# The first expert layer of a two-layer attention and mixture-of-experts kernel: another order of chunks, a selection in two parts, one more wait on GpSimd, and two one-hot matrices written by ScalarE

## The chip, the cores and the metric

The kernel runs on one core of a Trainium2 chip. The metric is the device time of one execution in microseconds (us). The engines are TensorE (PE; PEld is its loading of weights), VectorE (DVE), ScalarE (ACT), GpSimd (POOL) and SyncE (SP), which here only issues DMAs.

## What is computed

There are 2048 tokens (8 x 256) of width 256, and four layers, each added to its input after a layer norm: attention over sets, a mixture of 16 experts with a shared one, an attention over context, and a mixture of 8 experts. The second layer is the one that most of the change touches:

```python
scores = jax.nn.sigmoid(x @ router_w.T)                       # 2048 x 16
_, topk_idx = jax.lax.top_k(scores + e_bias[None, :], 4)
topk_w = jnp.take_along_axis(scores, topk_idx, axis=1)
topk_w = topk_w / (topk_w.sum(axis=-1, keepdims=True) + 1e-20)
combine = jnp.zeros((T, 16)).at[jnp.arange(T)[:, None], topk_idx].add(topk_w)
for each expert e:  g, u = split(x @ gu_w[e].T);  routed += combine[:, e] * (silu(g) * u @ d_w[e].T)
shared = silu(x @ shared_gate_w.T) * (x @ shared_up_w.T) @ shared_down_w.T
```

In the fourth layer each token goes to two of eight experts. The kernel computes for each choice a slot in a table of 39 blocks of 128 rows, and from that the list of the rows that each block gathers.

## The kernel before

**The first experts.** The 16 experts of width 96 are laid side by side, 1536 columns, and cut into 12 chunks of 128; the shared expert is a 13th chunk of 96 (`C0` = 13). Tokens go in four groups of 512 (`NG`). In `ffn0_group(g, k)` TensorE does for each chunk `c`: a small matmul that spreads the weights of the chosen experts over the chunk's 128 hidden rows (`spread`, into bank 4, L1108), then `up0` of the next chunk (12 matmuls of 512 columns, since each product is made of three, high x high, high x low and low x high: L1065 to L1067), then `down0` of this chunk (12 matmuls of 256 columns). Between `up0` and `down0` of a chunk stand ScalarE's silu (L806), VectorE's product with the up part (L1589), its product with the spread weights (L1594; not for the shared chunk, which comes last), the rounding to the high part (L1599) and the two halves of the low part (L1603).

**The weights of the choice.** Before the first group's loop VectorE chooses, in one row of 15 dependent steps, four of sixteen experts for all 16 tiles of 128 tokens (`dve.max`, `dve.match_replace`, normalising, and a split of each weight in three bf16 parts, `c3`; L1545 to L1574). TensorE, having done `up0(0, 0, 0)`, waits for that (`b_c3`), turns `c3` (16 transposes, L1121), ScalarE copies the four results (`cT`, L796), and only then does the loop start.

**Low parts of the weights and inputs.** GpSimd makes them (`gate_low`, `down_low0`, `low_rows`): L535, L548, L542. `GU_PART` and `DN_PART` say which columns go in which piece, in the order in which chunks need them.

**Weights of the last layer.** Beside the first experts the weights of the last layer are split in 68 parts of 512 columns: SyncE loads a part, ScalarE rounds it (`high_part`, L817), GpSimd subtracts (`low_part`, L577), SyncE stores both. ScalarE's order is fixed: in the first group parts 0 and 1 come behind the silu of chunk 0, part 2 behind that of chunk 1, part 3 behind that of chunk 2, parts 4 and 5 behind that of chunk 3. `high_part(n)` waits until the low part `n - 2` is made (`p_lo`) and the high part `n - 2` is stored (`hi_out`). GpSimd makes its first low part only behind all of the work of the paragraph above.

**Slots in the last layer.** For eight batches of four columns VectorE writes small matrices `placed` (L1777) and, in one instruction of 512 columns, four one-hot matrices (L1780); TensorE multiplies them (L1303). What it sums is the list by which GpSimd fetches rows (L667).

What sets the order is the program of each engine, written by hand; semaphores tie them.

## Time and profile before

| | us |
|---|---|
| median of 3 runs | 760.92 |
| lowest, highest | 759.76, 761.35 |
| the profiled execution | 759.37 |
| its span, first to last instruction | 757.6 |
| TensorE busy in it | 697.8 (92%) |
| VectorE, ScalarE, GpSimd busy | 480.2, 253.1, 332.3 |

The profiled execution is 1.8 us longer than its span, and 1.55 us shorter than the median. The first experts run from about 83 to 347 us of the span, the choice of slots from about 456 to 474 us, the last experts from 480 us to the end.

### The profile page before, as it was taken

The numbers are of one execution on the slowest core, as the hardware profiler recorded it, in microseconds if no ns is written. First come the engines' busy times: TensorE is split into PE (matmuls) and PEld (weight loads), VectorE is DVE, ScalarE is ACT, GpSimd is POOL, SyncE is SP. The second block draws the span as 40 slices with busy tenths as digits, with TensorE's granted clock in tenths as the row PEclk, the third lists the DMA queues.
The fourth block names the chain that finished last, engine by engine and source line by source line (L and its number), as shares of the span: only waits on it lengthen the run. The fifth ranks groups of instructions, "written<-read, shape, count | busy, mean of one in ns | idle before, by whom it ended". The sixth has DMA issues, their size and how long they took to land.

```text
span 757.6 us, 14725 instructions
## 1 busy us (share of the span) xinstructions
PE 697.8 (92%) x4707; PEld 622.5 (82%) x4707; DVE 480.2 (63%) x1322; ACT 253.1 (33%) x474; POOL 332.3 (44%) x324
## 2 busy tenths in 40 slices
PE   4999679999999999998899995699999999999996
PEld 3868558878888888887677784599999999999995
DVE  5969956667667677766699958344444444454443
ACT  1367233222322232335556640132323323233231
POOL 6236943434344334335512115345554655455553
PEclk9997569999999999999999995699999999999998
DMA  8901036766667766747950028522445355434221
GB/s 219 332 2 32 25 119 214 241 219 222 206 221 237 232 202 207 256 158 300 430 153 30 29 66 308 159 36 44 107 90 154 50 155 161 148 58 146 44 37 21
DMA packets 60265, 114.95 MB, mean 152 GB/s; under 512 B 15185, under 2 KB 29394, under 8 KB 57778
## 3 DMA queue, kind: packets, MB, share of 16 engines
q1 hardware_dynamic: 50514, 103.48, 40.1%
q0 software_dynamic: 8736, 10.39, 8.4%
q8 instruction: 37, 0.61, 0.3%
q10 hardware_dynamic: 960, 0.33, 0.2%
q14 instruction: 18, 0.15, 0.1%
HBM read 68.89 MB, written 45.29 MB: 151 GB/s over the span
## 4 chain that ended last, share of the span: by engine, by line
PE 78%; DVE 14%; issue 4%; ACT 2%; DMA 1%; POOLq 0%; POOL 0%; DVEq 0%
PE ps L1065 19%; PE ps L1066 18%; PE ps L1067 18%; PE ps L1335 3%; PE ps L1192 2%; PE ps L1183 2%; PE ps L1229 2%; PE ps L1108 1%; PE ps L937 1%; PE ps L1314 1%; PE ps L1205 1%; DVE h_high L1599 1%; DVE h_low L1603 1%; PE ps L1140 1%; PE ps L1221 1%
## 5 line engine op out<-in xcount | busy, mean ns | idle before, releaser
L577 POOL TENSOR_TENSOR part_lo<-wexp,part_hi 128x512 fp32r<-128x512 f32 x68 | 89.3, 1323 | 133.6 <-ACT part_hi L817 131.3
L684 POOL DMA_INDIRECT out_rows<-vbd,slot_row x39 | 63.3, 1623 | 107.4 <-DVE vbd L1819 75.7
L1065 PE MATMUL ps<-w_hi,x_high 128*128 x312 | 105.1, 337 | 1.1 <-DVE x_low L1824 1.1
L1066 PE MATMUL ps<-up_low,x_high 128*128 x312 | 101.6, 326 | 0.0
L1067 PE MATMUL ps<-w_hi,x_low 128*128 x312 | 101.6, 326 | 0.0
L1840 DVE TENSOR_TENSOR arena<-arena,ps 128x704 f32<-128x704 f32 x39 | 34.6, 888 | 103.1 <-ACT arena L905 86.9
L1065 PE MATMUL ps<-xn_high,gu_high 128*128 (+3 forms) x208 | 93.0, 447 | 0.1
L806 ACT ACTIVATE wexp<-ps 128x512 f32<-128x512 f32 (+1 forms) x52 | 31.1, 597 | 160.4 <-PE ps L1067 160.3
L1066 PE MATMUL ps<-xn_low,gu_high 128*128 (+3 forms) x208 | 82.9, 399 | 0.0
L1067 PE MATMUL ps<-xn_high,gu_low 128*128 (+3 forms) x208 | 82.7, 397 | 0.0
L517 POOL TENSOR_TENSOR rstd<-ve,mhalf 128x2 f32<-128x2 f32 (+1 forms) x31 | 22.3, 719 | 110.3 <-DVE ve L1397 110.3
L905 ACT ACTIVATE arena<-ps 128x704 f32<-128x704 f32 x39 | 29.6, 759 | 119.6 <-PE ps L1067 72.2
L1065 PE MATMUL ps<-dn_high,h_high 128*128 128x256 f32 (+1 forms) x208 | 61.3, 295 | 4.5 <-DVE h_low L1603 4.5
L1065 PEld LDWEIGHTS ps<-w_hi,x_high 128*128 128x128 f32 x312 | 59.8, 192 | 1.5 <-issue 1.5
L1065 PE MATMUL ps<-w_hi,hT_high 128*128 x195 | 58.7, 301 | 2.0 <-DVE hT_high L1833 2.0
L1589 DVE TENSOR_TENSOR wexp<-wexp,ps 128x512 f32<-128x512 f32 (+1 forms) x52 | 35.7, 686 | 39.0 <-ACT wexp L806 38.8
L1066 PEld LDWEIGHTS ps<-up_low,x_high 128*128 128x128 f32 x312 | 59.8, 192 | 0.0
L1067 PEld LDWEIGHTS ps<-w_hi,x_low 128*128 128x128 f32 x312 | 59.6, 191 | 0.0
L1066 PE MATMUL ps<-dn_low,h_high 128*128 128x256 f32 (+1 forms) x208 | 58.8, 283 | 0.0
L1067 PE MATMUL ps<-dn_high,h_low 128*128 128x256 f32 (+1 forms) x208 | 58.6, 282 | 0.0
L1603 DVE TENSOR_TENSOR h_low<-wexp,h_high 128x256 fp32r<-128x256 f32 (+1 forms) x104 | 55.4, 574 | 1.8
L1067 PE MATMUL ps<-w_hi,hT_low 128*128 x195 | 55.6, 285 | 0.0
(287 smaller groups left out, 1693.2 us busy)
## 6 DMA issues: line engine op xcount, KB each, us to landing
wexp<-in_wexp SPq DMA_DIRECT2D x68, 256.0 KB, 3.2
w_hi_rows<-part_hi SPq DMA_DIRECT2D x68, 256.0 KB, 2.6
w_lo_rows<-part_lo SPq DMA_DIRECT2D x68, 256.0 KB, 2.1
w_hi<-w_hi_rows SPq DMA_DIRECT2D x8, 2048.0 KB, 19.0
up_low<-w_lo_rows SPq DMA_DIRECT2D x8, 1408.0 KB, 6.0
down_low<-w_lo_rows SPq DMA_DIRECT2D x8, 768.0 KB, 8.3
wexp<-in_gu SPq DMA_DIRECT2D x2, 1632.0 KB, 10.8
xn_rows<-arena SPq DMA_DIRECT2D x8, 256.0 KB, 2.1
```

Source lines behind the costliest of these rows:

```text
L517: pool.tensor_tensor(rstd[:, bass.ds(b * TB, TB)], ve[:, bass.ds(b * TB, TB)], mhalf[:, 0:1].broadcast_to([P, TB]), ALU.pow).then_inc(ln_r ...
L577: pool.tensor_tensor(part_lo[:, n % 2, :], part_w[:, n % 4, :], part_hi[:, n % 2, :].bitcast(F32), ALU.subtract).then_inc(p_lo, 1)
L684: pool.indirect_dma_start(out=out_rows, out_offset=bass.IndirectOffsetOnAxis(ap=slot_row[:, i:i + 1], axis=0), in_=yb[:, i % 2, :], in_off ...
L806: act.activation(sg0[0:rows, c % 2, :], bank(c % 2)[0:rows, :], ACT.Silu).then_inc(b_silu, 1)
L905: act.activation(sg1.rearrange("p (a n) -> p a n", a=2), bank(0, 2).rearrange("p (a n) -> p a n", a=2)[:, :, 0:HALF1], ACT.Silu).then_inc( ...
L1065: pe.matmul(out, high, rows_high, start=start, stop=False, skip_group_check=True)
L1066: pe.matmul(out, high, rows_low, start=False, stop=False, skip_group_check=True)
L1067: return pe.matmul(out, low, rows_high, start=False, stop=stop, skip_group_check=True)
L1335: mm = pe.transpose(bank(4, 2)[:, c * P:(c + 1) * P], h1[:, c * P:(c + 1) * P], ident[:, :])
L1589: dve.tensor_tensor(hm0[0:rows_, c % 2, :], sg0[0:rows_, c % 2, :], bank(2 + c % 2)[0:rows_, :], ALU.mult).then_inc(b_prod, 1)
L1603: dve.tensor_tensor(h_low[0:rows_, c % 2, cols], hm0[0:rows_, c % 2, cols], h_high[0:rows_, c % 2, cols].bitcast(F32), ALU.subtract).then_ ...
L1840: dve.tensor_tensor(h1[:, 0:I1].rearrange("p (a n) -> p a n", a=2), sg1.rearrange("p (a n) -> p a n", a=2), bank(2, 2).rearrange("p (a n) ...
```

## The change

1. **Order of chunks.** In every group the shared chunk (96 rows, no weights) comes first, then experts' chunks 9, 10, 11, then 6 to 8, 3 to 5, 0 to 2 (`chunk_of`). `GU_PART`, `DN_PART` and `down_high0` follow that order: the first piece of the gate and up weights has 960 columns where it had 768, the last 768 where it had 960.
2. **Choice in two parts.** VectorE chooses for tiles 0 to 3 (group 0) ahead of the chunks; for the other twelve tiles the steps are put behind chunks 0 to 7 of group 0 (`select_rest`). TensorE turns the weights of group 0 behind `up0(0, 1)`, those of groups 1 and 2 behind chunk 8, those of group 3 behind chunk 10; ScalarE's copies are set in its row of silus.
3. **GpSimd** waits for the first part of the choice (`b_c3`) before it goes on with low parts.
4. **One-hots.** Those of batches 2 and 5 are made by ScalarE: four `Abs(inblock - iota)` of 128 columns and one `Relu(1 - .)` of 512.

**GpSimd between the norm and the first parts of the last layer's weights.** `xn_low`, `gu_low` and `dn_low` are the low parts; `part_lo` is the last layer's. Before:

```order
L542 TENSOR_TENSOR xn_low<-wexp,xn_high 128x2x256 [waits b_routed] x2
L535 TENSOR_TENSOR gu_low<-wexp,gu_high 128x960 [waits w_high]
L548 TENSOR_TENSOR dn_low<-wexp,dn_high 128x768 [waits w_high]
L535 TENSOR_TENSOR gu_low<-wexp,gu_high 128x960 [waits w_high]
L548 TENSOR_TENSOR dn_low<-wexp,dn_high 128x768 [waits w_high]
L542 TENSOR_TENSOR xn_low<-wexp,xn_high 128x2x256 [waits b_routed] x3
L577 TENSOR_TENSOR part_lo<-wexp,part_hi 128x512 [waits p_hi] x2
```

and now:

```order
L554 TENSOR_TENSOR xn_low<-wexp,xn_high 128x2x256 [waits b_routed,b_c3]
L554 TENSOR_TENSOR xn_low<-wexp,xn_high 128x2x256 [waits b_routed]
L547 TENSOR_TENSOR gu_low<-wexp,gu_high 128x768 [waits w_high]
L560 TENSOR_TENSOR dn_low<-wexp,dn_high 128x768 [waits w_high]
L547 TENSOR_TENSOR gu_low<-wexp,gu_high 128x768 [waits w_high]
L560 TENSOR_TENSOR dn_low<-wexp,dn_high 128x768 [waits w_high]
L554 TENSOR_TENSOR xn_low<-wexp,xn_high 128x2x256 [waits b_routed] x3
L590 TENSOR_TENSOR part_lo<-wexp,part_hi 128x512 [waits p_hi] x2
```

The wait for `b_c3` stands ahead of nine low parts, two of them shorter by 192 columns, and ahead of the first `part_lo`.

**ScalarE from the sigmoid to the third silu.** The first `ACTIVATE` is the sigmoid of the scores, `arena<-ps 96x512` a copy of turned weights, `wexp<-ps` a silu, `part_hi` a rounding of a part. Before:

```order
L793 ACTIVATE arena<-ps 128x256 [waits b_routed]
L796 ACTIVATE arena<-ps 96x512 [waits b_turned] x4
L806 ACT_TABLE_LOAD
L806 ACTIVATE wexp<-ps 128x512 [waits b_up]
L817 ACTIVATE part_hi<-wexp 128x512 [waits p_in0]
L817 ACTIVATE part_hi<-wexp 128x512 [waits p_in1]
L806 ACTIVATE wexp<-ps 128x512 [waits b_up]
L817 ACTIVATE part_hi<-wexp 128x512 [waits p_lo,hi_out0,p_in2]
L806 ACTIVATE wexp<-ps 128x512 [waits b_prod,b_up]
```

and now:

```order
L806 ACTIVATE arena<-ps 128x256 [waits b_routed]
L819 ACT_TABLE_LOAD
L819 ACTIVATE wexp<-ps 96x512 [waits b_up]
L810 ACTIVATE arena<-ps 96x512 [waits b_turned]
L837 ACTIVATE part_hi<-wexp 128x512 [waits p_in0]
L837 ACTIVATE part_hi<-wexp 128x512 [waits p_in1]
L819 ACTIVATE wexp<-ps 128x512 [waits b_up]
L837 ACTIVATE part_hi<-wexp 128x512 [waits p_lo,hi_out0,p_in2]
L819 ACTIVATE wexp<-ps 128x512 [waits b_prod,b_up]
```

Three of the four copies have gone from here; the part that waits for `p_lo` still stands ahead of the third silu.

**VectorE from the scores to the first chunk.** `MAX`, `MATCH_REPLACE` and what follows are the choice; `ps 96x512` and `h_high`, `h_low` belong to the shared chunk. Before:

```order
L1554 MATCH_REPLACE arena<-t,arena 128x20 x15
L1556 SCALAR_TENSOR_TENSOR arena<-arena 128x256 [waits b_max]
L1559 TENSOR_REDUCE sums<-arena 128x16 [waits b_step]
L1561 TENSOR_SCALAR sums<-sums 128x16 [waits b_step]
L1563 RECIPROCAL recs<-sums 128x16 [waits b_step]
L1565 TENSOR_TENSOR arena<-arena,recs 128x256 [waits b_step]
L1568 CAST arena<-arena 128x16x16 [waits b_step]
L1570 TENSOR_TENSOR arena<-arena 128x256 [waits b_c3]
L1572 CAST arena<-arena 128x16x16 [waits b_step]
L1574 TENSOR_TENSOR arena<-arena 128x16x16 [waits b_c3]
L1589 TENSOR_TENSOR wexp<-wexp,ps 128x512 [waits b_silu]
L1594 TENSOR_TENSOR wexp<-wexp,ps 128x512 [waits b_spread,b_prod]
```

and now:

```order
L1626 TENSOR_REDUCE sums<-arena 128x4 [waits b_step]
L1628 TENSOR_SCALAR sums<-sums 128x4 [waits b_step]
L1630 RECIPROCAL recs<-sums 128x4 [waits b_step]
L1611 TENSOR_TENSOR arena<-arena,recs 128x64 [waits b_step]
L1634 CAST arena<-arena 128x4x16 [waits b_step]
L1636 TENSOR_TENSOR arena<-arena 128x64 [waits b_c3]
L1638 CAST arena<-arena 128x4x16 [waits b_step]
L1640 TENSOR_TENSOR arena<-arena 128x4x16 [waits b_c3]
L1695 TENSOR_TENSOR wexp<-wexp,ps 96x512 [waits b_silu]
L1705 CAST h_high<-wexp 96x512 [waits b_prod]
L1709 TENSOR_TENSOR h_low<-wexp,h_high 96x256 [waits b_high]
L1709 TENSOR_TENSOR h_low<-wexp,h_high 96x256
```

Each instruction of the choice has a quarter of its columns, and the first chunk's product, cast and subtractions follow at once, with no product with spread weights between.

```diff
+        def chunk_rows(q):
+            return P if q else I0
+        def chunk_of(q):
+            return 9 - (q - 1) // 3 * 3 + (q - 1) % 3 if q else C0 - 1
-        GU_PART = [slice(0, 3 * 2 * P), slice(3 * 2 * P, 6 * 2 * P), slice(6 * 2 * P, 9 * 2 * P), slice(9 * 2 * P, GU0)]
-        DN_PART = [slice(0, 4), slice(4, 7), slice(7, 10), slice(10, C0)]
+        GU_PART = [slice(9 * 2 * P, GU0), slice(6 * 2 * P, 9 * 2 * P), slice(3 * 2 * P, 6 * 2 * P), slice(0, 3 * 2 * P)]
+        DN_PART = [slice(9, C0), slice(6, 9), slice(3, 6), slice(0, 3)]
...
             gate_low(5)
+            pool.wait_ge(b_c3, 3)
             for n in range(3, 5):
                 low_rows(n)
...
                     act.activation(sg0[0:rows, c % 2, :], bank(c % 2)[0:rows, :], ACT.Silu).then_inc(b_silu, 1)
+                    if k == 0 and c == 0:
+                        copy_weights(0)
+                    if k == 0 and c == 9:
+                        copy_weights(1)
+                        copy_weights(2)
+                    if k == 0 and c == 11:
+                        copy_weights(3)
...
+            for m, n in enumerate(ACT_HOTS):
+                for j in range(BATCH):
+                    c = n * BATCH + j
+                    act.activation(gaps[:, m, j, :], iota[:, :], ACT.Abs, scale=-1.0,
+                                   bias=inblock[:, :, :].rearrange("p w t -> p (w t)")[:, c:c + 1]).then_inc(hot_step, 1)
+                act.wait_ge(hot_step, (BATCH + 1) * m + BATCH)
+                if n >= NBUF:
+                    act.wait_ge(d_placed, n - NBUF + 1)
+                act.activation(onehot[:, n % NBUF, :, :], gaps[:, m, :, :], ACT.Relu, scale=-1.0, bias=1.0).then_inc(hot_step, 1)
...
+                for c in range(C0):
+                    if c:
+                        if k == 0 and c == 1:
+                            pe.wait_ge(b_cT, 1)
+                            pe.wait_ge(pool_step, 13)
+                        else:
+                            pe.wait_ge(b_mult, g * (C0 - 1) + c - 1)
+                        pe.matmul(bank(4), spread[:, chunk_of(c) * P:(chunk_of(c) + 1) * P], cT[:, bass.ds(g * 512, 512)],
+                                  start=True, stop=True).then_inc(b_spread, 1)
+                    if c < C0 - 1:
+                        up0(g, c + 1, k)
+                        if k == 0 and c == 0:
+                            turn_weights(0)
+                        down0(g, c, k)
+                    if k == 0 and c == 8:
+                        turn_weights(1)
+                        turn_weights(2)
+                    if k == 0 and c == 10:
+                        turn_weights(3)
...
             up0(0, 0, 0)
-            pe.wait_ge(b_c3, 3)
...
-            pe.wait_ge(b_cT, NG)
...
+            def select_rest(q):
+                if q == 0:
+                    biased(rest).then_inc(b_step, 1)
+                elif q == 1:
+                    dve.wait_ge(b_step, 11)
+                    for t in range(4, NT):
+                        largest(t)
...
-                    if c < C0 - 1:
-                        dve.wait_ge(b_spread, g * (C0 - 1) + c + 1)
+                    if c:
+                        dve.wait_ge(b_spread, g * (C0 - 1) + c)
...
+                if n not in ACT_HOTS:
+                    dve.tensor_tensor(onehot[:, n % NBUF, :, :], iota[:, :].unsqueeze(1).broadcast_to([P, BATCH, P]),
```

## Rows read from the trace of the kernel before

**Rows 1.** The page's chain that ended last: shares by engine.
```profile
PE 78%; DVE 14%; issue 4%; ACT 2%; DMA 1%; POOLq 0%; POOL 0%; DVEq 0%
```

**Rows 2.** Stretches: PE, PEld, DVE, ACT, POOL busy (count); PE clock, DMA share, GB/s.
```profile
83.00:88.00 5.00, 4.88 (x13) 3.51 (x12) 4.41 (x38) 0.38 (x1) 5.00 (x4) 0.58 0.01 3
...
88.00:99.00 11.00, 0.00 (x0) 0.00 (x0) 10.69 (x24) 0.00 (x0) 10.62 (x7) 0.62 0.00 0
...
103.00:108.00 5.00, 5.00 (x13) 3.49 (x12) 3.55 (x5) 2.33 (x4) 2.69 (x2) 0.53 0.33 110
...
108.00:160.00 52.00, 51.40 (x290) 43.66 (x290) 33.07 (x58) 14.96 (x27) 18.65 (x15) 1.00 0.71 232
```

**Rows 3.** Timeline, VectorE at the start of the experts (start, us).
```profile
83.49 0.64 DVE L1545 TENSOR_TENSOR arena<-arena,ebias 128x256 f32<-128x256 f32 x1 [0.75 <-ACT arena L793]
...
84.16 1.39 DVE L1549 MAX8 m<-arena 128x8 f32<-128x20 f32 x16
...
86.58 0.09 DVE L1554 MATCH_VALUE_LOAD arena<-t,arena 128x8 f32 x1
...
89.08 1.65 DVE L1556 SCALAR_TENSOR_TENSOR arena<-arena 128x256 f32<-128x256 f32 x1
...
91.21 1.60 DVE L1561 TENSOR_SCALAR sums<-sums 128x16 f32<-128x16 f32 x1
...
98.80 0.42 DVE L1574 TENSOR_TENSOR arena<-arena 128x256 bf16<-128x256 f32 x1
```

**Rows 4.** Timeline, GpSimd in the same stretch.
```profile
83.80 2.69 POOL L542 TENSOR_TENSOR xn_low<-wexp,xn_high 128x512 fp32r<-128x512 f32 x2
...
86.46 2.23 POOL L535 TENSOR_TENSOR gu_low<-wexp,gu_high 128x960 fp32r<-128x960 f32 x1
...
88.64 1.80 POOL L548 TENSOR_TENSOR dn_low<-wexp,dn_high 128x768 fp32r<-128x768 f32 x1
...
94.51 4.11 POOL L542 TENSOR_TENSOR xn_low<-wexp,xn_high 128x512 fp32r<-128x512 f32 x3
```

**Rows 5.** Timeline, the opening of the first group on three engines.
```profile
87.49 0.40 PE L1067 MATMUL ps<-xn_high,gu_low 128*128 128x512 f32 x1
...
99.28 1.09 PE L1121 MATMUL ps<-identb,arena 128*96 128x128 bf16 x8 [11.39 <-DVE arena L1574]
...
104.34 0.69 DVE L1589 TENSOR_TENSOR wexp<-wexp,ps 128x512 f32<-128x512 f32 x1 [5.12 <-ACT wexp L806]
...
108.05 0.60 ACT L806 ACTIVATE wexp<-ps 128x512 f32<-128x512 f32 x1 [2.71 <-PE ps L1067]
...
116.91 0.28 PE L1065 MATMUL ps<-dn_high,h_high 128*128 128x256 f32 x1
```

**Rows 6.** DMA issues of the page: size, median us to landing.
```profile
w_hi_rows<-part_hi SPq DMA_DIRECT2D x68, 256.0 KB, 2.6
...
w_lo_rows<-part_lo SPq DMA_DIRECT2D x68, 256.0 KB, 2.1
```

**Rows 7.** Timeline, a small VectorE instruction with GpSimd idle of SBUF work.
```profile
458.64 0.23 DVE L1746 TENSOR_TENSOR vbd<-vbd,small 128x64 f32<-128x64 f32 x1
```

**Rows 8.** Timeline, VectorE and GpSimd taking turns in group one.
```profile
206.98 2.75 POOL L577 TENSOR_TENSOR part_lo<-wexp,part_hi 128x512 fp32r<-128x512 f32 x2 [4.98 <-ACT part_hi L817]
...
207.18 2.82 DVE L1603 TENSOR_TENSOR h_low<-wexp,h_high 128x256 fp32r<-128x256 f32 x2
```

**Rows 9.** Timeline, TensorE after the first change of group.
```profile
167.87 0.39 PE L1065 MATMUL ps<-dn_high,h_high 128*128 128x256 f32 x1 [0.89 <-DVE h_low L1603]
```

**Rows 10.** Timeline, placing the rows in slots.
```profile
470.41 0.76 DVE L1777 SCALAR_TENSOR_TENSOR placed<-blkno,column,rowval 128x40 fp32r<-128x40 f32 x4
...
471.10 0.68 DVE L1780 TENSOR_TENSOR onehot<-iota,inblock 128x512 fp32r<-128x512 f32 x1
...
471.70 0.76 DVE L1777 SCALAR_TENSOR_TENSOR placed<-blkno,column,rowval 128x40 fp32r<-128x40 f32 x4
...
473.21 1.01 PE L1303 MATMUL ps<-placed,onehot 128*128 128x40 f32 x4 [0.27 <-DVE onehot L1780]
```

More of the change, by code:

```diff
@@ L1069, in up0 @@
             def up0(g, c, k):
-                i, rows = g * C0 + c, P if c < C0 - 1 else I0
-                if k == 0 and c in (3, 6, 9):
-                    pe.wait_ge(w_low, 2 * (c // 3 + 1))
+                i, rows = g * C0 + c, chunk_rows(c)
+                if k == 0 and c in (4, 7, 10):
+                    pe.wait_ge(w_low, 2 * ((c - 1) // 3 + 1))
                 if k or c >= 2:
@@ L1544, in _, with biased @@
             dve.wait_ge(b_sig, 1)
-            dve.tensor_tensor(sel0[:, :, 0:E0], sc0, ebias[:, :].unsqueeze(1).broadcast_to([P, NT, E0]),
-                              ALU.add).then_inc(b_step, 1)
+            first, rest = slice(0, 4), slice(4, NT)
+            def biased(tiles):
+                n = tiles.stop - tiles.start
+                return dve.tensor_tensor(sel0[:, tiles, 0:E0], sc0[:, tiles, :],
+                                         ebias[:, :].unsqueeze(1).broadcast_to([P, n, E0]), ALU.add)
@@ new lines, in largest, with marked, chosen_scores, normalised @@
+            def largest(t):
+                dve.max(m8[:, t, :], sel0[:, t, :]).then_inc(b_max, 1)
+            def marked(t):
+                dve.match_replace(rep0[:, t, :], t8[:, t, :], sel0[:, t, :], FOUND).then_inc(b_max, 1)
+            def chosen_scores(tiles):
+                return dve.scalar_tensor_tensor(out=cw0[:, tiles, :], in0=rep0[:, tiles, 0:E0], scalar=1.0e38,
+                                                in1=sc0[:, tiles, :], op0=ALU.is_gt, op1=ALU.mult)
+            def normalised(tiles):
+                n = tiles.stop - tiles.start
+                return dve.tensor_tensor(cw0[:, tiles, :], cw0[:, tiles, :],
+                                         recs[:, tiles].unsqueeze(2).broadcast_to([P, n, E0]), ALU.mult)
@@ L1555, in _ @@
-            dve.wait_ge(b_max, 2 * NT)
-            dve.scalar_tensor_tensor(out=cw0, in0=rep0[:, :, 0:E0], scalar=1.0e38, in1=sc0,
-                                     op0=ALU.is_gt, op1=ALU.mult).then_inc(b_step, 1)
+            for t in range(4):
+                marked(t)
+            dve.wait_ge(b_max, 8)
+            chosen_scores(first).then_inc(b_step, 1)
             dve.wait_ge(b_step, 5)
-            dve.tensor_reduce(sums[:, :], cw0, AX.X, ALU.add).then_inc(b_step, 1)
+            dve.tensor_reduce(sums[:, first], cw0[:, first, :], AX.X, ALU.add).then_inc(b_step, 1)
@@ L1760, in _ @@
             step(dve.tensor_scalar(column[:, :, :], column[:, :, :], ROUND, ROUND, ALU.add, ALU.subtract))
[L1761 to L1762 removed]
+            dve.scalar_tensor_tensor(out=inblock[:, :, :], in0=column[:, :, :], scalar=-float(P),
+                                     in1=place[:, :, :], op0=ALU.mult, op1=ALU.add).then_inc(in_known, 1)
+            dve.wait_ge(in_known, 1)
             dve.wait_ge(pool_slot, 6)
```

123 lines of the change are left out of this document (78 added, 45 removed).

## The prediction

> **What bounds the kernel now.** I read the chain of waits first: TensorE holds 78% of it, VectorE 14% [rows 1]. So a change pays where TensorE stands still, and little elsewhere. The stretches [rows 2] show the largest such place: from 88 to 99 us TensorE does nothing, while VectorE is busy for 10.69 of 11 us, and after it the granted clock is 0.53 (1.2 GHz) from 103 to 108 us; from 108 us on TensorE is busy for 51.40 of 52 us at 1.00 (2.4 GHz). What fills the gap is the choice of experts: its first step starts at 83.49 us and its last ends at 98.80 + 0.42 = 99.22 us [rows 3]; TensorE's last matmul of the first chunk ends at 87.9, its transposes start at 99.28 after 11.39 us idle, and the third chunk's down matmuls start at 116.91 [rows 5]. I measure the change at that last point, because all that is new in the opening stands before it.
>
> The choice is long because GpSimd works beside it. A subtraction of a constant on 16 columns takes 1.60 us there [rows 3], a product of 64 columns 0.23 us with GpSimd at small work [rows 7]. VectorE's copies, casts and products of two SBUF tensors end with the ends of GpSimd's instructions (90.40, 92.75, 94.51; rows 4 show the first starts and lengths) [rows 3, 4]. In group one two subtractions take 2.82 us across two GpSimd instructions that take 2.75 [rows 8]. So I count: such a VectorE instruction costs its own time alone, and waits out one GpSimd instruction where they are back to back.
>
> **The change part by part**, in the time frame of the trace.
>
> *Selection of four tiles.* GpSimd stands still from its wait to the end of it. Scores 0.64 (its row, GpSimd still at work); 4 maxima at 1.39/16 plus a handover, 0.42; 4 match steps at (89.08 - 86.58)/16, 0.62; 5 products or sums at 0.23 + 0.04 handover, 1.35; 4 copies, casts or constants at 0.22, 0.9; a reciprocal 0.28. Sum 4.2 us [rows 3, 7], so it ends at 87.7, about when the first chunk's matmuls do. TensorE goes on with the second chunk instead of waiting.
>
> *The backlog of GpSimd.* What it did from 83.80 on now starts at 87.7: five low parts of inputs at 1.35 to 1.37 (6.8 us) and four of weights, all of 768 columns, at 1.80 (7.2 us) [rows 4]. That is 14.0 us, to 101.7. Only then comes the first low part of the last layer's weights, 1.3 us, to 103.0. ScalarE's second rounding behind chunk 1 waits for it, and the silu of chunk 2 is queued behind that rounding. So TensorE's lead is taken back here: rounding 0.6 and silu 0.6 [rows 5] give 104.2, VectorE's product 0.69 [rows 5] and the same again for the weights 105.7, cast 0.43 and first subtraction 0.38 give 106.5 alone, 107.8 if one of them waits out a GpSimd instruction of 1.3. I take 107.1. Before it was 116.91: **9.8 us less**. TensorE's own work up to there (two rounds of 4.41 from 92.3, which is when the first subtraction of the shared chunk can be ready) would allow 101.9 with VectorE's waits, so the cover for VectorE's extra work of the first two chunks is this 5 us; it costs nothing there.
>
> *Norm before it.* The first two gate pieces have 192 more columns; GpSimd takes 2.23 for 960 and 1.80 for 768 [rows 4], and the scales of the norm are queued behind them. Between 0 and 0.9; I take **+0.4**, since VectorE idles in part of that stretch.
>
> *Transposes in the loop.* Twelve of the sixteen stand behind chunks 8 and 10. Eight took 1.09 us at the low clock [rows 5]: twelve 1.6 at that, half at the full one. **+0.9**. ScalarE's three copies lie beside matmuls (0.6 each against a round of 4.41).
>
> *Selection of twelve tiles in rounds 2 to 7.* VectorE is busy 33.07 of 52 us in group 0 [rows 2], so 1.6 us of a round of 4.41 are free, and a piece is 0.6 to 1.0 us alone. Nine of the pieces' instructions can wait out 1.3 us each. Between 0 and 4; **+0.5**, because the free time is nearest to the pieces' own length.
>
> *Clock.* TensorE will work about 60% of the time from 91 to 107. Before, after an idle of 11.39 us, it ran at 1.2 GHz up to about 107.3. At 1.2 GHz a round lasts twice, so some 4 us of work cost 2. Between 0 and 2.1; **+0.9**.
>
> *Changes of group.* At each of three, TensorE idles 0.89 [rows 9], because VectorE first adds the group's result and then takes the first chunk through two products. Now that chunk has one product less, 0.69, and TensorE one small matmul (0.23) less to cover it with; the cast may meet GpSimd. **-0.35** each, **-1.0** in all (0 to -1.4). The last chunk, now with the product, has queries ahead of its down matmuls as cover: 0.
>
> *One-hots.* A batch costs VectorE 471.70 - 470.41 = 1.29 us, of which the one-hot is 0.60 [rows 10]; TensorE follows with 1.01 per batch, so it doesn't become the bound. Two fewer: **-1.2**. ScalarE needs at most five instructions of 0.60 per batch: 3.0 us, ready at 464.9 and 467.9, wanted at 465.8 and 469.2. What follows is a gather through GpSimd; 0 if that is held by another DMA, so 0 to -1.2.
>
> Sum: -9.8 + 0.4 + 0.9 + 0.5 + 0.9 - 1.0 - 1.2 = **-9.3 us**. The profiled execution of 759.37 would be 750.1; the median lies 1.55 above the profiled one, so the forecast is 760.9 - 9.3 = **751.6**.
>
> **A rule against the trace.** In rows 8 three VectorE instructions lengthen a pair of GpSimd's from 2.6 to 2.75, so 0.05 each. The Trainium skill, "SBUF — State Buffer", section "Who interferes with whom", says that the port pair of the two engines is an exclusive lock held for the whole instruction, and the other engine blocks fully. By that each of the seven such VectorE instructions of chunks 0 and 1 would push GpSimd's backlog back by its whole length, and the sum would be that of the first rival, 754.6.
>
> **The rivals.**
> - *The backlog grows.* If GpSimd waits out VectorE's seven casts and subtractions (0.43 each), part 0 is ready 3.0 us later and so is chunk 2: 754.6. For it: these engines do take turns. Against it: the 2.75 us of rows 8.
> - *VectorE becomes the bound in rounds 2 to 7.* Each piece waits out GpSimd and free time doesn't hold it: 3 us more than I took, 754.6. For it: two parts in a round are frequent. Against it: 1.6 us free per round.
> - *No hold at chunk 2.* If GpSimd's backlog doesn't hold ScalarE, chunk 2's down matmuls start at 101.9, 5.2 us earlier: 746.4. For it: nothing but that the trace of before never shows this wait. Against it: the order of ScalarE's program.
> - *Slower: the parts become the bound.* Part n + 2 needs part n stored. Rounds of 4.41 with 17 parts in 13 chunks ask for one in 3.37 us. Before, the loop began with GpSimd free and the parts were ahead; now the chunks start ahead of them. Rounding 0.6, low part 1.3, issue, and landing in 2.6 and 2.1 us [rows 6] make some 5.5 us for two, 2.7 for one, which is under 3.37. If one took 4.4, 14 parts at 1.0 each cost 14 us more, and the kernel takes 765.6. It decides from 0.67 us per part over 3.37.
> - *The choice of four tiles isn't in time* because its waits for semaphores are longer than 0.04: each us costs one us of all this, still faster.
>
> **How the numbers follow.** Forecast 0.65; grown backlog 0.11; VectorE as the bound 0.12; no hold 0.05; parts as the bound 0.04; something that takes all of the gain back 0.03. The lower end joins the best bounds of the unknown costs (clock, pieces, norm at 0, chunk 2 at 106.5: -11.7) and part of the way to "no hold"; the upper end takes in both cases at 754.6 with 1.4 us for their own terms: 747.5 to 756.0. A measurement of this kernel can tell about 0.2% (1.5 us) from no change. Faster by more than that 0.93, within 0.03, slower 0.04.
>
> **What would show it.** Right: TensorE's idle time of 11.39 us gone and several short ones before about 107 us; ScalarE's third rounding ending near 103.6, its releaser GpSimd's first `part_lo` after a POOL row without a gap from 88 to 103; VectorE's choice of four tiles done at 87.7; chunk 2's down matmuls at 107; eight batches of placing done 1.2 us sooner. Wrong: a silu of chunk 2 at 98 (no hold); backlog ending after 104; rounds 2 to 7 longer than 4.6 us with `h_low` as releaser; a granted clock of 0.5 after 110 us. The forecast fails as a whole if the parts fall behind for more than the first four.

## Result and profile after

The change makes the kernel faster by about 1.5%.

| | before | after |
|---|---|---|
| median of four runs, us | 761.13 (759.76 to 764.67) | 750.53 (749.71 to 751.65) |
| ratio after / before | | 0.9855 (95% interval 0.9818 to 0.9891) |
| profiled execution, us (span) | 759.37 (757.6) | 750.95 (749.2) |

The forecast was 751.6 us, in a range of 747.5 to 756.0. The profiled executions differ by 8.4 us, the medians by 10.6. The page of after, its engines, the clock in 40 slices and the chain by engine:

```profile
PE 699.1 (93%) x4707; PEld 623.5 (83%) x4707; DVE 478.3 (64%) x1331; ACT 257.1 (34%) x484; POOL 333.2 (44%) x324
...
PEclk9996589999999999999999995799999999999999
...
PE 80%; DVE 10%; issue 4%; POOL 2%; ACT 2%; DMA 1%; SPq 0%; POOLq 0%; DVEq 0%
```

VectorE's share of the chain falls from 14% to 10% and GpSimd, which had 0% [rows 1], now has 2%. Stretches that answer to [rows 2], counted from a sigmoid that comes 5.4 us later (columns as there):

```profile
88.00:99.00 11.00, 8.83 (x37) 6.50 (x36) 8.88 (x27) 4.37 (x7) 6.22 (x4) 0.81 0.07 25
99.00:113.00 14.00, 11.07 (x45) 9.04 (x46) 11.11 (x24) 1.12 (x2) 12.14 (x9) 0.78 0.25 78
113.00:160.00 47.00, 46.63 (x272) 39.81 (x273) 36.44 (x85) 16.33 (x29) 18.74 (x14) 1.00 0.76 257
```

The 11 us without a matmul are gone: TensorE is busy for 8.83 of the first 11 us, and for 11.07 of the 14 that follow. From 113 us on it is as full as it was before from 108 us (46.63 of 47 us at full clock). VectorE now carries 36.44 of 47 us there, with the twelve tiles' selection in it.

Timeline of after, VectorE at the start of the experts. These rows answer to [rows 3]:

```profile
88.92 0.22 DVE L1596 TENSOR_TENSOR arena<-arena,ebias 128x64 f32<-128x64 f32 x1 [2.65 <-ACT arena L806]
89.18 0.42 DVE L1600 MAX8 m<-arena 128x8 f32<-128x20 f32 x4
...
91.08 0.17 DVE L1628 TENSOR_SCALAR sums<-sums 128x4 f32<-128x4 f32 x1
...
91.50 0.23 DVE L1611 TENSOR_TENSOR arena<-arena,recs 128x64 f32<-128x64 f32 x1
...
92.47 0.23 DVE L1640 TENSOR_TENSOR arena<-arena 128x64 bf16<-128x64 f32 x1
...
95.64 3.88 DVE L1709 TENSOR_TENSOR h_low<-wexp,h_high 96x256 fp32r<-96x256 f32 x2
99.44 1.97 DVE L1596 TENSOR_TENSOR arena<-arena,ebias 128x192 f32<-128x192 f32 x1
...
103.41 2.82 DVE L1709 TENSOR_TENSOR h_low<-wexp,h_high 128x256 fp32r<-128x256 f32 x2
```

The choice of four tiles runs from 88.92 to 92.70 us. The last three rows are VectorE's work beside GpSimd: the pair of subtractions takes 0.76 us where it meets none of GpSimd's work (as at 112.38 us), here 3.88 and 2.82.

GpSimd in the same stretch answers to [rows 4], and ScalarE and TensorE to [rows 5] (the number in brackets is the idle time before the row and what ended it):

```profile
92.78 2.54 POOL L554 TENSOR_TENSOR xn_low<-wexp,xn_high 128x512 fp32r<-128x512 f32 x2 [5.64 <-DVE arena L1640]
95.29 1.99 POOL L547 TENSOR_TENSOR gu_low<-wexp,gu_high 128x768 fp32r<-128x768 f32 x1
...
103.05 4.34 POOL L554 TENSOR_TENSOR xn_low<-wexp,xn_high 128x512 fp32r<-128x512 f32 x3
107.35 2.53 POOL L590 TENSOR_TENSOR part_lo<-wexp,part_hi 128x512 fp32r<-128x512 f32 x2
```

```profile
97.28 0.58 ACT L819 ACTIVATE wexp<-ps 128x512 f32<-128x512 f32 x1
108.74 0.63 ACT L837 ACTIVATE part_hi<-wexp 128x512 fp32r<-128x512 f32 x1 [10.89 <-POOL part_lo L590]
109.28 0.58 ACT L819 ACTIVATE wexp<-ps 128x512 f32<-128x512 f32 x1
```

```profile
97.70 0.36 PE L1096 MATMUL ps<-dn_high,h_high 96*128 96x256 f32 x1 [1.99 <-DVE h_low L1709]
99.57 0.58 PE L1096 MATMUL ps<-dn_high,h_high 96*128 96x256 f32 x1 [0.74 <-DVE h_low L1709]
...
112.86 0.39 PE L1096 MATMUL ps<-dn_high,h_high 128*128 128x256 f32 x1 [2.36 <-DVE h_low L1709]
...
163.58 0.39 PE L1096 MATMUL ps<-dn_high,h_high 96*128 96x256 f32 x1 [0.40 <-DVE h_low L1709]
```

GpSimd waits 5.64 us for the choice and then works through its backlog, 92.78 to 107.35, without a gap. Only then comes the first low part of the last layer's weights. ScalarE waits 10.89 us for it with a rounding at the head of its queue, and the third silu (109.28) is queued behind that. The third chunk's down matmuls start at 112.86 us. The last row is the first change of group, where TensorE idles 0.40 us; before it was 0.89 [rows 9].

At the end of the experts' choice of slots (VectorE; `m`, the first step of placing, then `slot_row`, the last) and ScalarE's part in it:

```profile
448.34 0.29 DVE L1837 TENSOR_REDUCE m<-arena 128x16 f32<-128x128 f32 x1
...
467.70 0.26 DVE L1894 TENSOR_SCALAR slot_row<-ps,norow 128x39 int32<-128x39 f32 x1 [1.20 <-PE ps L1349]
```

```profile
456.32 1.28 ACT L920 ACTIVATE vbd<-iota,inblock 128x128 f32<-128x128 f32 x4 [9.42 <-DVE inblock L1869]
457.63 0.63 ACT L925 ACTIVATE onehot<-vbd 128x512 fp32r<-128x512 f32 x1
```

**Where the 8.4 us come from.** I follow the same five events through both traces: ScalarE's sigmoid (which opens the choice), the first add of a group's result on VectorE, the fourth one, `m`, and `slot_row`, and after them the first silu of the last experts.

| stretch | before, us | after, us | difference |
|---|---|---|---|
| start to sigmoid | 83.07 | 88.51 | +5.4 |
| sigmoid to first add | 81.11 | 72.09 | -9.0 |
| first to fourth add (three groups) | 182.78 | 180.98 | -1.8 |
| fourth add to `m` (attention) | 106.74 | 106.76 | 0 |
| `m` to `slot_row` | 20.56 | 19.36 | -1.2 |
| `slot_row` to first silu of the last experts | 13.05 | 11.78 | -1.3 |
| first silu to the end | 270.3 | 269.7 | -0.6 |

The second row is more than the forecast gave, the first is a loss that it put at 0.4.

### The profile page after: what moved, and what is told of

Same layout as the page of the kernel before. It is cut to its first block, busy times and chain, and to the rows that moved or that the text cites. A ratio compares the mean times of both kernels' runs of the same rounds, so it can differ in the third digit from the quotient of the medians.

```text
span 749.2 us, 14748 instructions
## 1 busy us (share of the span) xinstructions
PE 699.1 (93%) x4707; PEld 623.5 (83%) x4707; DVE 478.3 (64%) x1331; ACT 257.1 (34%) x484; POOL 333.2 (44%) x324
## 4 chain that ended last, share of the span: by engine, by line
PE 80%; DVE 10%; issue 4%; POOL 2%; ACT 2%; DMA 1%; SPq 0%; POOLq 0%; DVEq 0%
PE ps L1096 18%; PE ps L1097 18%; PE ps L1098 18%; PE ps L1381 3%; PE ps L1235 2%; PE ps L1226 2%; PE ps L968 2%; PE ps L1272 2%; PE ps L1032 2%; PE ps L1023 2%; PE ps L1143 1%; DVE h_low L1709 1%; PE ps L1360 1%; PE ps L1248 1%; PE ps L1183 1%
## 5 line engine op out<-in xcount | busy, mean ns | idle before, releaser
L1709 DVE TENSOR_TENSOR h_low<-wexp,h_high 128x256 fp32r<-128x256 f32 (+1 forms) x104 | 66.1, 676 | 1.8
L1097 PE MATMUL ps<-down_low,hT_high 128*128 x195 | 55.0, 282 | 0.0
```

What stands on the lines that cost most here:

```text
L1097: pe.matmul(out, high, rows_low, start=False, stop=False, skip_group_check=True)
L1709: dve.tensor_tensor(h_low[0:rows_, c % 2, cols], hm0[0:rows_, c % 2, cols], h_high[0:rows_, c % 2, cols].bitcast(F32), ALU.subtract).then_ ...
```

## Experiments

All kernels below are compared with the kernel before, run beside them. The ratios are therefore comparable from one table row to the next, but where their intervals overlap they rank nothing. The spans and stretches come from one profiled execution of each. "Chunk 2" is the time from the sigmoid to the third chunk's first down matmul. The last column gives, in us, where the granted clock falls to 1.2 GHz before the sigmoid and, after a "/", around 360 us ("-": no such fall).

| kernel | ratio (95%) | span | sigmoid at | chunk 2 | sigmoid to first add | falls |
|---|---|---|---|---|---|---|
| before | | 757.6 | 83.07 | 33.84 | 81.11 | 67 / - |
| before_again | | 757.0 | 85.39 | 33.31 | 80.57 | 28, 66 / - |
| before_wide | 1.0024 (0.9990 to 1.0057) | 759.1 | 88.52 | 31.22 | 78.48 | 61 / 371 |
| after | 0.9855 (0.9818 to 0.9891) | 749.2 | 88.51 | 24.35 | 72.09 | 61 / - |
| after_again | | 747.1 | 83.81 | 24.55 | 74.54 | 66 / - |
| even_pieces | 0.9874 (0.9852 to 0.9896) | 750.3 | 85.42 | 25.42 | 73.58 | 25, 66 / 363 |
| no_gpsimd_wait | 0.9893 (0.9868 to 0.9917) | 752.7 | 88.56 | 25.60 | 73.25 | 61 / 365 |
| choice_whole | 0.9953 (0.9920 to 0.9986) | 756.7 | 88.67 | 30.74 | 79.59 | 25, 62 / - |
| two_parts_early | 0.9836 (0.9776 to 0.9895) | 748.4 | 86.64 | 22.17 | 70.98 | 28, 62 / - |
| no_act_one_hots | 0.9893 (0.9848 to 0.9939) | 749.0 | 88.58 | 24.35 | 71.64 | 61 / - |
| backlog_spread | 0.9847 (0.9814 to 0.9880) | 749.1 | 88.52 | 20.00 | 69.55 | 61 / 361 |
| spread_again | | 746.7 | 85.76 | 20.39 | 69.94 | 66 / 359 |
| spread_even | 0.9810 (0.9770 to 0.9850) | 747.8 | 88.18 | 21.10 | 71.07 | 61 / - |

### GpSimd doesn't wait

Of after, one line is taken out, so that GpSimd works beside the choice of four tiles:

```diff
-            pool.wait_ge(b_c3, 3)
```

> The changed kernel without GpSimd's wait for the choice of the first four tiles. If the wait is what keeps the choice short: the choice, 3.8 us long now, takes 10 to 13 us, since nine of its instructions wait out one of GpSimd's each, and TensorE stands still for 5 to 8 us ahead of the transposes; GpSimd's backlog ends 3.5 us earlier, so the third silu can come at 105.5 instead of 109.3. If the opening is set by VectorE: 2 to 5 us slower, 752.5 to 755.5. If it is set by the backlog alone: 3 us faster, 747.5.

Timeline of this kernel, steps of the choice on VectorE and then GpSimd:

```profile
88.98 0.77 DVE L1595 TENSOR_TENSOR arena<-arena,ebias 128x64 f32<-128x64 f32 x1 [2.65 <-ACT arena L805]
...
93.62 1.46 DVE L1627 TENSOR_SCALAR sums<-sums 128x4 f32<-128x4 f32 x1
...
95.33 1.58 DVE L1610 TENSOR_TENSOR arena<-arena,recs 128x64 f32<-128x64 f32 x1
...
100.57 0.22 DVE L1639 TENSOR_TENSOR arena<-arena 128x64 bf16<-128x64 f32 x1
```

```profile
96.77 3.72 POOL L554 TENSOR_TENSOR xn_low<-wexp,xn_high 128x512 fp32r<-128x512 f32 x3
102.74 2.55 POOL L589 TENSOR_TENSOR part_lo<-wexp,part_hi 128x512 fp32r<-128x512 f32 x2 [2.25 <-ACT part_hi L836]
```

The choice of the same four tiles takes 11.8 us (88.98 to 100.79) instead of 3.8. A constant added on 4 columns takes 1.46 us instead of 0.17, a product of 64 columns 1.58 instead of 0.23. So the reading of [rows 3, 4] holds: the choice is long because of what runs beside it, however few columns it has. But chunk 2 comes only 1.25 us later (25.60 instead of 24.35), since GpSimd is through at 100.49 and, at 102.74, waits for ScalarE instead of ScalarE for it. The two orders put the same conflict in two places: GpSimd's wait makes the choice 8 us shorter and the backlog's end 6.9 us later (3.5 had been expected). The silu of chunk 2 waits here for TensorE, not for the backlog, and TensorE runs at half clock from 98 to 109 us, so part of the 1.25 us may be the clock's. The wait is worth 1.2 us in the profile (73.25 against 72.09 to the first add). The ratios, 0.9893 against 0.9855, point the same way, with intervals that overlap.

### The whole choice at once

Here all sixteen tiles are chosen ahead of the first product, as before the change, but in the new order of chunks, and GpSimd waits to the end:

```diff
-            pool.wait_ge(b_c3, 3)
+            pool.wait_ge(b_c3, 6)
...
+            for q in range(8):
+                select_rest(q)
...
-                    if k == 0:
-                        select_rest(c)
```

> The changed kernel with the choice for the other twelve tiles directly behind the first four, ahead of the chunks, and GpSimd waiting for all of it. By the prediction's count of VectorE's steps (5 to 6 us alone) the shared chunk's product and GpSimd's backlog both start that much later, and the third silu with them: 5 to 6 us more than the changed kernel, 755.5 to 756.5, from the sigmoid to the first addition 77 to 78 us. Rival (the twelve tiles cost as much in rounds 0 to 7, where they meet GpSimd, as ahead of them): within 1.5 us of 750.5.

TensorE's rows of this kernel with what they waited for:

```profile
102.56 0.55 PE L1096 MATMUL ps<-dn_high,h_high 96*128 96x256 f32 x1 [6.11 <-DVE h_low L1712]
...
119.41 0.39 PE L1096 MATMUL ps<-dn_high,h_high 128*128 128x256 f32 x1 [3.87 <-DVE h_low L1712]
```

ScalarE's third rounding and the silu of chunk 2 behind it:

```profile
115.29 0.63 ACT L837 ACTIVATE part_hi<-wexp 128x512 fp32r<-128x512 f32 x1 [16.68 <-POOL part_lo L590]
115.83 0.58 ACT L819 ACTIVATE wexp<-ps 128x512 f32<-128x512 f32 x1
```

VectorE goes through all sixteen tiles in 10.3 us (89.08 to 99.39), with GpSimd still. The first down matmuls come at 102.56 instead of 97.70, and chunk 2 is 6.4 us later than in after, the first add 7.5 us later, against 5 to 6 expected. About 1.1 of the 7.5 us arise behind chunk 2, where this execution is at half clock once more, from 120 to 123 us. The ratio, 0.9953, lies clear of after's 0.9855. That is the largest effect of any one part that was undone: choosing for one group ahead and for the rest behind the chunks brings 6.4 of the 9.5 us at chunk 2. The rows show the way it takes: GpSimd waits for the choice, so its backlog starts 6.7 us later (99.47 instead of 92.78), and ScalarE's hold is 16.68 us instead of 10.89. What the whole choice would cost with GpSimd let go earlier wasn't tried.

### The hold at chunk 2

GpSimd's first two low parts of the last layer's weights are put behind `gate_low(6)`, that is ahead of the last six of the nine pieces of the backlog (the later parts begin at part 2; not shown):

```diff
             gate_low(6)
+            low_part(0)
+            low_part(1)
             down_low0(2)
...
```

> The changed kernel with GpSimd's first two low parts of the last layer's weights put behind the third of its nine waiting low parts, so that ScalarE's rounding ahead of the third silu is released at about 99 us instead of 108.7. Theory of the hold (the backlog of GpSimd sets the third chunk): the third silu at 99 to 100 us instead of 109.3, the third chunk's down matmuls 4 to 5 us earlier than 112.9, and 745.5 to 747. Rival (VectorE, which waits out GpSimd at each cast and subtraction, is as late as the silu): less than 1.5 us gained, 749 to 750.5.

```profile
97.32 0.63 ACT L841 ACTIVATE part_hi<-wexp 128x512 fp32r<-128x512 f32 x1 [1.36 <-POOL part_lo L576]
...
98.83 1.80 DVE L1709 CAST h_high<-wexp 128x512 fp32r<-128x512 f32 x1
...
100.67 3.90 DVE L1713 TENSOR_TENSOR h_low<-wexp,h_high 128x256 fp32r<-128x256 f32 x2
101.70 0.60 ACT L823 ACTIVATE wexp<-ps 128x512 f32<-128x512 f32 x1 [3.75 <-PE ps L1102]
```

These are ScalarE and VectorE of this kernel. The wait of 10.89 us shrinks to 1.36, and the silu of chunk 2 waits for TensorE (3.75 us) instead. So the hold is what the prediction said it was, and without it chunk 2 is 2.2 us earlier (22.17 against 24.35), not the 5.2 us that the rival "no hold" had allowed. What is late next is VectorE behind chunk 1: a cast of 1.80 and two subtractions of 3.90 us, against 0.43 and 0.76 without GpSimd beside them. At the first add 1.1 us of the gain are left (70.98 against 72.09).

The next kernel spreads twelve low parts over the backlog, one or two between GpSimd's other pieces (the order begins: parts 0 and 1, gate piece 6, part 2, down piece 2, part 3, gate piece 7):

```diff
+            low_part(0)
+            low_part(1)
             gate_low(6)
+            low_part(2)
             down_low0(2)
+            low_part(3)
             gate_low(7)
...
```

> The changed kernel with GpSimd's nine waiting low parts spread over the chunks of group 0: first two low parts of the last layer's weights, then one waiting piece behind each one or two of them. From the sigmoid to the first addition of a group's result the changed kernel takes 72.1 us, the one with two parts early 71.0, where the hold of ScalarE was gone but VectorE's casts and subtractions of chunks 0 and 1 still waited out GpSimd. If that contention is what is left: those five instructions take 3 us for a chunk instead of 5 to 6, the way takes 67 to 69 us, and the kernel 745 to 747.5. Rival (what is left is VectorE's own work and the clock): 70 to 71 us, 748 to 750.

ScalarE of this kernel:

```profile
99.02 0.63 ACT L851 ACTIVATE part_hi<-wexp 128x512 fp32r<-128x512 f32 x1 [1.10 <-DMA w_hi_rows<-part_hi]
100.24 0.60 ACT L833 ACTIVATE wexp<-ps 128x512 f32<-128x512 f32 x1 [0.59 <-PE ps L1112]
...
107.30 0.60 ACT L833 ACTIVATE wexp<-ps 128x512 f32<-128x512 f32 x1 [4.06 <-PE ps L1112]
```

Nothing on ScalarE waits for GpSimd any more. Chunk 2 comes 4.35 us earlier than in after (20.00), the first add 2.5 us (69.55 against 72.09). A second execution, spread_again, repeats this with 20.39 and 69.94:

> The kernel with the spread backlog once more. If its start of the second attention (2.5 us earlier than in the changed kernel, beside the same weight loads) sets the clock's fall at 361 us: again there, and again 2.6 us for it. If executions differ: no fall there, and 748 us.

The first add comes later than the 67 to 69 us expected if the contention was all that was left, and earlier than the rival's 70 to 71. Part of the gain is given back: from chunk 2 to the first add both executions take 49.55 us at full clock, against 47.74 in after, and TensorE waits for `h_low` there three times, 0.60, 0.17 and 0.69 us in backlog_spread. The work put off meets VectorE later. In the whole time neither kernel is shown to be faster than after: the intervals, 0.9776 to 0.9895 and 0.9814 to 0.9880, hold after's 0.9855.

### ScalarE's one-hots

ScalarE writes no one-hot here; VectorE writes all eight, as before the change:

```diff
-        ACT_HOTS = (2, 5)
+        ACT_HOTS = ()
```

> The changed kernel with all one-hot matrices written by VectorE again. By the prediction's term: two instructions of 0.60 us back in the row, 1.2 us more, 751.7, and from the reduction `m` before the slots to `slot_row` 14.4 us instead of 13.24. Rival (the gather waits for another DMA anyway): no difference behind `slot_row`, 750.5.

```profile
447.58 0.29 DVE L1837 TENSOR_REDUCE m<-arena 128x16 f32<-128x128 f32 x1
...
468.12 0.26 DVE L1894 TENSOR_SCALAR slot_row<-ps,norow 128x39 int32<-128x39 f32 x1 [1.20 <-PE ps L1349]
```

On VectorE it is 20.54 us from the first to the second row; in after 19.36, in before 20.56. The two one-hots are worth 1.2 us, twice 0.6. From `slot_row` to the first silu of the last experts it takes 11.93 us, in after 11.78, so nothing of it is given back there. The spans (749.0 and 749.2) and the ratios, whose intervals overlap, are too coarse to show it.

### The 5.4 us ahead of the sigmoid

The sigmoid comes 5.4 us later in after than in before, with hardly anything changed ahead of it but the width of the first weight pieces. The first theory was that these wide pieces (GpSimd rounds 960 columns first) delay the norm. Two kernels test it: before with the wide first piece (960 columns), and after with a narrow one (704 columns, the last piece 1024), which takes an order of chunks of its own:

```diff
-        GU_PART = [slice(0, 3 * 2 * P), slice(3 * 2 * P, 6 * 2 * P), slice(6 * 2 * P, 9 * 2 * P), slice(9 * 2 * P, GU0)]
+        GU_PART = [slice(0, 960), slice(960, 1728), slice(1728, 2496), slice(2496, GU0)]
```

> The kernel before with one part of the change alone: the first piece of the gate and up weights is 960 columns wide instead of 768, the last 768 instead of 960. In the changed kernel the sigmoid of the scores stands at 88.5 us instead of 83.1, and TensorE's granted clock falls at about 61 us instead of 67. Theory A (the wider pieces stand in front of the norm's scales on ScalarE and GpSimd, shift the mix and turn steps, and the clock falls earlier): the sigmoid comes at 87 to 89 us and the kernel takes 4 to 6 us longer than before, 765 to 767. Theory B (where the clock falls does not hang on the pieces): the sigmoid at 83 to 84 us, at most 1 us longer than before.

```diff
-            return 9 - (q - 1) // 3 * 3 + (q - 1) % 3 if q else C0 - 1
+            return (C0 - 1, 10, 11, 7, 8, 9, 4, 5, 6, 0, 1, 2, 3)[q]
-        GU_PART = [slice(9 * 2 * P, GU0), slice(6 * 2 * P, 9 * 2 * P), slice(3 * 2 * P, 6 * 2 * P), slice(0, 3 * 2 * P)]
+        GU_PART = [slice(10 * 2 * P, GU0), slice(7 * 2 * P, 10 * 2 * P), slice(4 * 2 * P, 7 * 2 * P), slice(0, 4 * 2 * P)]
...
```

> The changed kernel with other pieces: shared chunk and chunks 10 and 11 in the first piece (704 columns), then 7 to 9, 4 to 6, 0 to 3, and the waits that belong to it. Theory A (wide first pieces cost 5 us in the norm): the sigmoid back at 83 to 84 us and about 5 us less than the changed kernel, 745 to 746.5. Theory B: the clock still falls at about 61 us, within 1 us of the changed kernel's 750.5.

(Left out: the waits that follow this order.) The profiles seemed to bear it out: before_wide has its sigmoid at 88.52, like after, and even_pieces at 85.42. The whole times didn't: before_wide's ratio of 1.0024 is 1.8 us where 4 to 6 were expected, and even_pieces, expected at 745 to 746.5 us, has a ratio of 0.9874, no better than after's. And a row shows that it isn't GpSimd's work that is longer. These are the five us from 61 on, first of before, then of after:

```profile
61.00:66.00 5.00, 5.00 (x37) 4.17 (x35) 4.83 (x20) 4.00 (x7) 2.03 (x3) 1.00 0.00 0
```

```profile
61.00:66.00 5.00, 5.00 (x18) 3.87 (x18) 2.81 (x13) 2.72 (x5) 3.36 (x3) 0.50 0.00 0
```

TensorE is busy all the time in both, but does 37 matmuls at 2.4 GHz in one and 18 at 1.2 GHz in the other. The clock falls at 67 us in before and at 61 in after. ScalarE's rows show where the 5.4 us arise. The norm's eight batches each begin with a copy out of TensorE's bank (`wexp<-ps`), and this is the fourth of them, in before and in after:

```profile
66.04 0.60 ACT L784 ACTIVATE wexp<-ps 128x512 f32<-128x512 f32 x1 [0.47 <-PE ps L937]
```

```profile
71.54 0.60 ACT L797 ACTIVATE wexp<-ps 128x512 f32<-128x512 f32 x1 [2.75 <-PE ps L968]
```

The first of the eight comes 0.6 us later in after, the second 1.2, the fourth 5.5 and the eighth 5.4. From the second to the fourth it is 9.13 us instead of 4.83, and in after ScalarE waits 2.75 us for TensorE each time. So 4.3 of the 5.4 us are two batches at half clock that before does at full clock.

So the question became what sets that fall. Three more executions asked it: before and after once more, unchanged, and the spread order with the narrow first piece.

> The kernel before once more, to see where TensorE's granted clock falls in another execution and when the sigmoid comes. In three of four kernels with wide first pieces it fell at 61 or 62 us, in the one execution of the kernel before at 67. Theory A (wide pieces set it): again at 66 to 67, the sigmoid at 83.1. Theory B (it differs between executions): another place, the sigmoid at up to 88.5.

> The changed kernel once more. If the clock of a stage is set by what the program does there: falls at 61 us again, no fall between 340 and 400 us, sigmoid at 88.5, and 72 us from there to the first addition. If executions differ: another early fall at 25 to 28 us or one at 360 to 370.

The third is backlog_spread with this edit in it:

```diff
-            return 9 - (q - 1) // 3 * 3 + (q - 1) % 3 if q else C0 - 1
+            return (C0 - 1, 10, 11, 7, 8, 9, 4, 5, 6, 0, 1, 2, 3)[q]
-        GU_PART = [slice(9 * 2 * P, GU0), slice(6 * 2 * P, 9 * 2 * P), slice(3 * 2 * P, 6 * 2 * P), slice(0, 3 * 2 * P)]
+        GU_PART = [slice(10 * 2 * P, GU0), slice(7 * 2 * P, 10 * 2 * P), slice(4 * 2 * P, 7 * 2 * P), slice(0, 4 * 2 * P)]
...
```

> The changed kernel with GpSimd's waiting low parts spread over the chunks and the first pieces 704 columns wide. Narrow first pieces have had the granted clock fall at 66 or 67 us in all three kernels that have them, wide ones at 61 or 62 in all seven; the sigmoid came at 83.1 or 85.4 against 86.6 to 88.7. If that stands: the clock falls at 66 us or later, the sigmoid at 83 to 85.5 us, from there 69.6 us to the first addition as in the spread kernel, so 3 to 5 us less than it up to there. The end: 745 to 747.5 if the later stages run at the full clock, 748 to 750 if the clock falls for some us in the second attention (361 to 369 us), as in the spread kernel's profile.

The same five us of after_again, the same code as after, and then of spread_even, which has the narrow first piece:

```profile
61.00:66.00 5.00, 5.00 (x35) 4.08 (x33) 4.54 (x21) 4.24 (x8) 4.14 (x5) 1.00 0.00 0
```

```profile
61.00:66.00 5.00, 5.00 (x19) 4.13 (x20) 3.78 (x16) 2.43 (x4) 1.99 (x3) 0.50 0.00 0
```

With that the theory falls. After's own code, once more, holds full clock through 66 us and has its sigmoid at 83.81 us; the kernel with the narrow piece falls to half at 61. Over all profiles, wide pieces go with a fall at 61 or 62 us in seven and at 66 in two (after_again, spread_again), narrow ones (768 or 704 columns) with 66 or 67 in three and 61 in one. The place of the fall belongs to the execution, and whether the code shifts its odds can't be told from so few. Of the executions without an earlier fall at 25 or 28 us, those that fall at 61 have the sigmoid at 88.2 to 88.6, those that fall at 66 or 67 at 83.1, 83.8 and 85.8. The place of the fall isn't all of it. Up to the seventh batch after_again (80.07) and spread_again (80.08) run alike, and after is 2.8 us later (82.83). Then after_again's clock is full again from 80 to 83 us, and its sigmoid comes 1.95 us ahead of spread_again's.

A similar thing shows in the second attention. Rows of spread_again, then of spread_even (same columns):

```profile
355.00:372.00 17.00, 14.17 (x136) 11.05 (x135) 11.01 (x13) 8.11 (x12) 5.41 (x6) 0.80 1.01 431
```

```profile
355.00:372.00 17.00, 14.17 (x149) 11.37 (x148) 12.14 (x15) 9.93 (x18) 7.91 (x9) 1.00 1.01 430
```

In spread_again the clock is at 1.2 GHz from 359 to 366 us; backlog_spread has the same from 361 to 368. Both take 109.4 us from the fourth add to `m`; spread_even, like before and after, takes 106.4 to 106.8. So the 2.5 us that the spread order gains in the opening are mostly gone again in these two executions. A fall in this stretch, of 3 to 6 us, stands in before_wide, even_pieces and no_gpsimd_wait too.

## Why the prediction was right

**What bounds the kernel, and the measuring point.** Right. All that is new in the opening stands before the third chunk's down matmuls: sigmoid to that point was 33.84 us and is 24.35, 9.5 us less, where the terms of the sum for it gave 9.8.

**Selection of four tiles.** Forecast 4.2 us, measured 3.8. The small steps took 0.17 to 0.23 us, as the one row with GpSimd idle [rows 7] had let expect. (What the prediction calls a subtraction of a constant adds one, 1e-20; its time is read rightly.)

**Backlog of GpSimd.** Forecast 14.0 us from the end of the choice and then a hold on ScalarE, measured 14.6 (92.78 to 107.35), with the releaser that the prediction named. Two kernels show that it is the cause: two_parts_early takes the hold away and gains 2.2 us at chunk 2, backlog_spread 4.35. With the hold in place chunk 2 is the same at either clock: 24.35 us in after, at half clock from 98 to 105 us, and 24.55 in after_again, which is at full clock from 97 to 107. The half microsecond more is in pieces of 768 columns that took 1.94 to 2.00 us instead of 1.80, where VectorE's casts and subtractions lie beside them.

**The rule against the trace.** Beside the casts and subtractions of chunks 0 and 1 GpSimd's backlog took 0.6 us more than its rows of before add up to, some 0.1 for each of them, while the pairs of subtractions took 3.88 and 2.82 us instead of 0.76. The first rival, a backlog grown by 3.0 us, is out. The Trainium skill, "SBUF — State Buffer", section "Who interferes with whom", says of VectorE's two-port modes that whoever issues first gets the shared pair for the whole instruction and the other fully blocks. It counts casts there; of an instruction with two SBUF inputs, as the subtractions are, it says that it contends. For VectorE the trace agrees (an instruction waits out one of GpSimd's); for GpSimd, whose queue here is never empty, it doesn't: 0.1 us is not the 0.4 us that one of them lasts by itself.

**Transposes, selection of twelve tiles, clock.** Forecast +0.9, +0.5 and +0.9. From chunk 2's down matmuls to the first add, before takes 47.27 us and after 47.74, so +0.5 is all that is left behind chunk 2. In no_act_one_hots, the same code up to there, it is 47.29, so the first two terms, 1.4 us together, came to 0 to 0.5: they were taken too dear. The stretch at 1.2 GHz, 98 to 105 us, lies ahead of that point, where ScalarE's wait covers it. In after_again it comes again from 107 to 114 us, behind the hold, and the same stretch takes 49.99 us. So the clock's term is 0 in one execution and 2.3 us in the other (forecast 0.9, bounds 0 to 2.1). That VectorE didn't become the bound shows in 46.63 of 47 us on TensorE.

**Changes of group.** Forecast -1.0 (0 to -1.4), measured -1.8: -0.65, -0.65 and -0.50. TensorE's idle time went from 0.89 to 0.40 us, 0.49 of it, about what the term said; the rest of it I can't place. This term was mis-sized.

**One-hots.** Forecast -1.2, measured -1.2, and +1.18 where the part is undone.

**Norm.** This is the step that was wrong in the profile: forecast +0.4 with a bound of 0.9, measured +5.4. The working costed GpSimd's wider pieces alone. What it left out, in its terms for the norm and for the clock, is that the norm itself runs at either clock: before's 83.07 us is an execution in which the clock fell at 67, and after's fell at 61, which accounts for 4.3 of the 5.4. In after_again the sigmoid comes at 83.81, +0.7. The other execution of before (before_again, 85.39) shows that this mark moves in before too, by 2.3 us; a fall at 61 stands in neither of its two profiles. What the wider piece itself costs can't be told apart from this: between 0 and 0.9 fits, and 0.6 is what the first batch is late by.

**End of the stretch with the slots.** -1.3 us from `slot_row` to the first silu of the last experts wasn't in the sum. The clock came back at 477 us in after, at 487 in before. Between executions of one kernel this stretch differs as much (13.05 and 12.04 in before, 11.78 and 12.46 in after), so it is no gain of the change that I could show.

**The sum.** In the profiled pair a loss of 5.0 us ahead of the sigmoid that the sum didn't have stands against 4.2 us of gains that it didn't have either: 1.5 in the opening (9.0 for 7.5), 0.8 at the groups, 1.3 behind `slot_row` and 0.6 at the end. The nearness of 751.6 to the median of 750.53 is therefore in part luck. The pair before_again and after_again differs by 9.9 us in span, close to the forecast of 9.3: -1.6 ahead of the sigmoid, -6.0 to the first add (with after_again's slow clock in it), -1.7 in the groups, 0 in the attention, -1.2 at the placing, +0.4 and +0.2 behind it.

**The rivals.** "The parts become the bound" didn't come: TensorE is full from 113 us on (46.63 of 47). "No hold" was priced at 5.2 us; taking the hold away brought 2.2, spreading the whole backlog 4.35, of which 2.5 reached the first add.

**A faster version.** spread_even, the changed kernel with the low parts spread and the narrow first piece, has a ratio of 0.9810 to before (0.9770 to 0.9850), its six runs 744.51 to 751.32 us; after has 0.9855 (0.9818 to 0.9891). That is the lowest ratio measured, but the intervals overlap, so it isn't shown to be faster than after. Its runs scatter with the clock: those at a mean granted clock of 0.967 took 744.5 to 744.9 us, the one at 0.944 took 751.3.

**Open.** What sets where TensorE's clock falls at 25 or 28, at 61 or 66, and around 360 us, and whether before_wide costs anything (1.0024, 0.9990 to 1.0057). Nor is it settled whether the fall near 360 us has to do with the spread order: it stood in two of the three profiles of that order, and in three of the ten others. No kernel undoes the order of chunks alone: that the -1.8 us at the changes of group come from it is read from the rows (0.40 us idle instead of 0.89, behind the same `h_low`), not shown by an experiment.

## What to carry to other kernels

Where two engines take turns at a resource, letting one wait for the other mostly moves the cost: here the wait made the choice 8 us shorter and the end of GpSimd's backlog 6.9 us later, for a gain of 1.2. Follow the queue of the waiting engine to the first thing that a third engine needs from it, and put that first; here this brought 2.2 us at the next mark and 1.1 at the one after. Cut a long serial choice to what the next matmul needs, and hide the rest behind matmuls; here that was worth 6.4 us. And before a difference of some us ahead of the change is explained by the code, profile the same kernel a second time.
